# Odd tiles' x turned by VectorE and DRAM instead of TensorE, with the order around it changed, in a one-core Mamba2 layer

## What is computed

```python
xn = _layernorm(x, axis=-1)                      # x: 2 x 512 x 512
s = _L0_attn_ref(xn, in_proj_w, conv_w, conv_b, dt_bias, D, norm_w, out_proj_w)
g = _silu(_L0_ffn_ref(xn, w1, s1, w2, s2, w3, s3))
x = x + s * g
```

```python
xBC = jax.nn.silu(conv)                          # conv over the last 4 tokens
x, Bm, Cm = jnp.split(xBC, [INTER, INTER + NG * SS], axis=-1)
xdt = xc * dtc[..., None]
scores = jnp.einsum('bclhn,bcshn->bchls', Cc, Bc) * Lmat
Ydiag = jnp.einsum('bchls,bcshp->bclhp', scores, xdt)
states = jnp.einsum('bclhn,bchl,bclhp->bchpn', Bc, decay_states, xdt)
Yoff = jnp.einsum('bclhn,bchpn,bchl->bclhp', Cc, prev, jnp.exp(cs))
Y = (Ydiag + Yoff).reshape(Bsz, S, H, P) + x * D[None, None, :, None]
yg = y * jax.nn.silu(gate)
rstd = jax.lax.rsqrt(jnp.mean(jnp.square(yg_g), axis=-1, keepdims=True) + EPS)
```

## Time and profile before

| | |
|---|---|
| median of 3 runs | 1759.31 us (1758.42 to 1759.45) |
| the profiled execution | 1758.21 us, span of the core 1756.4 us |
| granted TensorE clock | 1.00 in the whole span |
| busy of the span | PE 99%, DVE 80%, ACT 70%, POOL 70% |
| DMA | 202.8 MB, mean 115 GB/s; SP's queue takes 34.8% of the 16 DMA engines |

### The profile page before, as it was taken

The page is one execution under the profiler, slowest core; times in us unless marked ns, Lnnn a source line. Parts: engine busy times, 40 slices in busy tenths (PEclk is TensorE's granted clock), DMA queues, the critical chain, the costliest instruction groups (busy, mean ns, idle before and its releaser), DMA issues.

```text
span 1756.4 us, 30305 instructions
## 1 busy us (share of the span) xinstructions
PE 1742.4 (99%) x10301; PEld 1459.3 (83%) x10301; DVE 1402.7 (80%) x2211; ACT 1221.6 (70%) x2456; POOL 1232.1 (70%) x877
## 2 busy tenths in 40 slices
PE   8999999999999999999999999999999999999999
PEld 6788888888888888888888888888888888888877
DVE  7978788878878788778788788878887887868941
ACT  6986677777776777777867778767877787643320
POOL 5677777777876787677776777677777787576630
PEclk9999999999999999999999999999999999999999
DMA  5442333333333343333333333333323343236522
GB/s 196 165 131 99 116 116 112 98 123 109 134 105 94 104 135 109 108 101 117 118 102 118 116 111 108 103 109 127 123 91 103 109 135 107 76 98 175 146 78 96
DMA packets 122595, 202.84 MB, mean 115 GB/s; under 512 B 23056, under 2 KB 60560, under 8 KB 122192
## 3 DMA queue, kind: packets, MB, share of 16 engines
q1 hardware_dynamic: 120720, 197.32, 34.8%
q10 hardware_dynamic: 1728, 3.65, 0.5%
HBM read 193.57 MB, written 7.34 MB: 114 GB/s over the span
## 4 chain that ended last, share of the span: by engine, by line
PE 94%; DVE 3%; issue 1%; POOL 1%; DMA 0%; ACT 0%; SPq 0%; DVEq 0%; ACTq 0%; POOLq 0%
PE bank L143 17%; PE bank L145 16%; PE bank L144 16%; PE bank L573 10%; PE bank L609 7%; PE bank L677 7%; PE bank L679 7%; PE bank L678 6%; PE bank L888 3%; PE bank L738 3%; DVE z L1246 1%; PE bank L700 0%; DVE lm L1267 0%; PE bank L720 0%; DVE acc L1337 0%
## 5 line engine op out<-in xcount | busy, mean ns | idle before, releaser
L964 ACT ACTIVATE lm<-lm,hp 128x128 f32<-128x128 f32 x1024 | 313.1, 389 | 0.8
L1246 DVE SCALAR_TENSOR_TENSOR z<-bank,cw_all,z 128x511 f32<-128x511 f32 (+2 forms) x384 | 286.9, 747 | 13.3 <-ACT z L1000 4.2
L1611 POOL TENSOR_TENSOR conv_lo<-raw_x,conv_hi 128x512 fp32r<-128x512 f32 x124 | 203.7, 1643 | 129.4 <-ACT conv_hi L901 129.3
L143 PE MATMUL bank<-xn_hi,conv_hi 128*128 128x512 f32 x640 | 261.4, 408 | 1.9 <-DVE z L1246 1.4
L1306 DVE TENSOR_TENSOR xdt<-bank,hp 128x512 f32<-128x512 f32 x128 | 88.2, 689 | 212.4 <-PE bank L738 212.4
L145 PE MATMUL bank<-xn_hi,conv_lo 128*128 128x512 f32 x640 | 250.6, 392 | 0.0
L144 PE MATMUL bank<-xn_lo,conv_hi 128*128 128x512 f32 x640 | 249.5, 390 | 0.0
L1594 POOL TENSOR_TENSOR yt<-yt,ec 128x384 f32<-128x384 f32 x128 | 146.8, 1147 | 139.3 <-DVE ec L1315 107.9
L1280 DVE SCALAR_TENSOR_TENSOR lm<-lm,gm 128x1024 f32<-128x1024 f32 x128 | 225.3, 1760 | 7.8 <-ACT lm L964 7.2
L1578 POOL TENSOR_TENSOR y_lo<-yt,y_hi 128x512 fp32r<-128x512 f32 x128 | 180.1, 1407 | 52.4 <-ACT y_hi L1035 52.4
L143 PE MATMUL bank<-xn_hi,gate_hi 128*128 128x512 f32 x512 | 212.9, 416 | 0.0
(11 more groups left out here) (152 smaller groups left out, 4051.5 us busy)
## 6 DMA issues: line engine op xcount, KB each, us to landing
lm<-cs_d SPq DMA_DIRECT2D x128, 512.0 KB, 4.5
raw_x<-w_conv_dram SPq DMA_DIRECT2D x128, 256.0 KB, 3.5
ec<-e_d SPq DMA_DIRECT2D x256, 96.0 KB, 2.7
raw_o<-w_out_dram SPq DMA_DIRECT2D x64, 256.0 KB, 3.0
raw_g<-w_gate_dram SPq DMA_DIRECT2D x61, 256.0 KB, 3.2
raw_g<-w_conv_dram SPq DMA_DIRECT2D x16, 256.0 KB, 3.2
raw_o<-w_conv_dram SPq DMA_DIRECT2D x14, 256.0 KB, 3.4
q_raw<-w1q_dram SPq DMA_DIRECT2D x10, 256.0 KB, 3.9
```

Source lines behind the costliest of these rows:

```text
L143: pe.matmul(dst, a_hi, b_hi, start=(i == 0), stop=False)
L964: e = act.activation(lm[m % LM_BUFS][:, u, :], lm[m % LM_BUFS][:, u, :], ACT.Exp, bias=hp[bd.seq][:, Q_CS, k1, u:u + 1])
L1246: dve.scalar_tensor_tensor(dst[:, d:SEQ], src[:, 0:SEQ - d], cw_all[:, bd.group, pos, 3 - d:4 - d], dst[:, d:SEQ], ALU.mult, ALU.add).then ...
L1611: pool.tensor_tensor(conv_lo[kx % 2][:, :, :], raw_x[:, kx % 2, :].rearrange("p (k j) -> p k j", k=KT), conv_hi[kx % 2][:, :, :].bitcast(F ...
```

## The change

Odd tiles from 7 to 123 (`by_blocks`) no longer go through `turn_x`. In step n - 2 DVE transposes the tile's `xt` in 32x32 blocks into `z[:, 1]`, SP stores that to a DRAM tensor `xb_d`, and in the step ahead of the tile's own SP loads it back in four DMAs of 32 partitions, in pieces of 32 floats, straight into `xdt[1]`, now with tokens on partitions. DVE computes `xw` from it and then scales it in place. In these odd steps t0 comes first on DVE and `scores` last, and PE's second diagonal waits for the state instead of `xw`. ACT waits for the store before it writes `z[:, 1]` anew. `sum_squares` moves from the end of step 0 to behind `y_off` of step 1, and the sums by token on DVE behind the block transpose of that step.

```diff
--- before.py
+++ after.py
@@ -47,6 +47,7 @@
 MREST = HIDDEN - MT * P
 
 LM_BUFS = 4
+BLK = P // 32
 
 SH = 4
 Q_BUFS = (2, 1, 1)
@@ -111,6 +112,16 @@
     return TILES // 2 <= n < TILES * (BODIES - 1) + TILES // 2
 
 
+def by_blocks(t):
+
+    return paired(t) and t % 2 == 1 and t >= TILES - 1
+
+
+def blocks_before(t):
+
+    return sum(1 for u in range(t) if by_blocks(u))
+
+
 def group_exists(group):
     return not isinstance(group, int) or 0 <= group < GROUPS
 
@@ -164,6 +175,7 @@
     cs_d = nc.dram_tensor("cs_d", (SEQS, HEADS, SEQ), F32).ap()
     e_d = nc.dram_tensor("e_d", (SEQS, HEADS, SEQ), F32).ap()
     hp_d = nc.dram_tensor("hp_d", (SEQS, P, NQ, GROUPS, TILES, 2 * NC), F32).ap()
+    xb_d = nc.dram_tensor("xb_d", (BLK, 32, NC, BLK, 32), F32).ap()
     mamba_d = nc.dram_tensor("mamba_d", (TT, P, DIM), F32).ap()
 
     with ExitStack() as ctx:
@@ -314,6 +326,7 @@
         ss_mm, rs_done, rv_done = sem("ss_mm"), sem("rs_done"), sem("rv_done")
         red_done = sem("red_done")
         tx_done = sem("tx_done")
+        blk_done, xb_out, xtok_in = sem("blk_done"), sem("xb_out"), sem("xtok_in")
         xdt_done, xw_done = sem("xdt_done"), sem("xw_done")
         min_done, exp_done, sc_done = sem("min_done"), sem("exp_done"), sem("sc_done")
         yd_done, yo_done = sem("yd_done"), sem("yo_done")
@@ -431,8 +444,23 @@
                                  cs_d[bd.seq, GH * bd.group + 2 * kr:GH * bd.group + 2 * kr + 2, :]
                                  .partition_broadcast(P)).then_inc(row_in[m % LM_BUFS], 16)
 
+            def blocks_out(t):
+                if by_blocks(t):
+                    sp.wait_ge(blk_done, blocks_before(t) + 1)
+                    wait(sp, xtok_in, 16 * BLK * blocks_before(t))
+                    sp.dma_start(xb_d.rearrange("g i c b j -> (g i) (c b j)"), z[:, 1, :]).then_inc(xb_out, 16)
+
+            def tokens_in(t):
+                if by_blocks(t):
+                    sp.wait_ge(xb_out, 16 * (blocks_before(t) + 1))
+                    sp.wait_ge(yd_done, t - 1)
+                    for b in range(BLK):
+                        sp.dma_start(xdt[1][32 * b:32 * b + 32, :].rearrange("i (c g j) -> i c g j", c=NC, g=BLK),
+                                     xb_d[:, :, :, b].rearrange("g i c j -> i c g j")).then_inc(xtok_in, 16)
+
             def step(body, k):
 
+                n = TILES * body.n + k
                 bx, kx = at(body, k, 5)
                 if bx.exists():
 
@@ -443,6 +471,7 @@
                 if k == 3 and nx.exists() and body.n > 0:
                     load_hp(nx)
                 load_rows(body, k)
+                blocks_out(n + 2)
                 bd, ke = at(body, k, 1)
                 if bd.exists():
 
@@ -453,6 +482,7 @@
                         sp.dma_start(ec[ke % 2][HD * j:HD * j + HD, :],
                                      e_d[bd.seq, GH * bd.group + 2 * ke + j, CHUNK:SEQ].partition_broadcast(HD)
                                      ).then_inc(ec_in[ke % 2], 16)
+                tokens_in(n + 1)
                 bd, k1 = at(body, k, 1)
                 for group, pos in out_piece(bd, k1):
                     wait(sp, wlo_o, TILES * group + pos)
@@ -615,7 +645,10 @@
                 n = TILES * body.n + k
                 pe.wait_ge(t0_done, n)
                 diag(n - 1, ps_y)
-                pe.wait_ge(xw_done, n + 1)
+                if by_blocks(n):
+                    pe.wait_ge(st_done, n)
+                else:
+                    pe.wait_ge(xw_done, n + 1)
                 diag(n, ps_x)
 
             def y_diag(body, k):
@@ -709,7 +742,7 @@
                         pe.wait_ge(t0_done, TILES * BODIES)
                         up(0, 0, P, 1, 1, 0)
                     if body.exists():
-                        wait(pe, gev_done, TILES * body.n + k + 3)
+                        wait(pe, gev_done, TILES * body.n + 3)
                     else:
                         wait(pe, st_done, TILES * BODIES)
                     if before.is_number(0):
@@ -731,7 +764,7 @@
             def turn_x(body, k):
                 n = TILES * body.n + k
                 bd, k1 = at(body, k, 1)
-                if bd.exists():
+                if bd.exists() and not by_blocks(n + 1):
                     pe.wait_ge(xs_done, TILES * bd.n + k1 + 1)
                     wait(pe, st_done, n + 1)
                     for c in range(NC):
@@ -740,6 +773,8 @@
 
             def step(body, k):
                 y_off(body, k)
+                if k == 1 and body.exists():
+                    sum_squares(body, 0)
                 conv(body, k)
                 if paired(TILES * body.n + k) and k % 2 == 0:
                     state_mm(body, k)
@@ -778,7 +813,8 @@
                     out_mm(body, k)
                 extra(body, k)
                 turn_x(body, k)
-                sum_squares(body, k)
+                if not body.exists():
+                    sum_squares(body, k)
 
             def turn(t):
                 pe.wait_ge(xn_done, t + 1)
@@ -997,6 +1033,8 @@
                     pos = X_POS[kx]
                     act.wait_ge(xp_done, m + 1)
                     wait(act, xs_done, m - 1)
+                    if by_blocks(m - 2):
+                        act.wait_ge(xb_out, 16 * (blocks_before(m - 2) + 1))
                     act.activation(z[:, kx % 2, :], ps_a[:, :], ACT.Identity, scale=cw_all[:, bd.group, pos, 3:4],
                                    bias=cw_all[:, bd.group, pos, 4:5]).then_inc(tap0_x, 1)
 
@@ -1286,8 +1324,8 @@
                 pv, kp = at(body, k, -1)
 
                 before = body.plus(-1)
-                if k == 1 and before.exists():
-
+
+                def sums_by_token():
                     dve.wait_ge(ss_mm, before.n + 1)
                     wait(dve, rv_done, before.n)
                     if body.exists():
@@ -1297,23 +1335,44 @@
                     dve.tensor_scalar(rstd_sum[:, :], tok_sum[:, :] if body.exists() else sums(before)[:, 0:NC], EPS,
                                       None, ALU.add).then_inc(rs_done, 1)
 
-                if body.exists():
-
-                    dve.wait_ge(tx_done, n + 1)
-                    if k == 0:
-                        wait_hp(dve, body)
-                    wait(dve, yd_done, n - 1)
-                    dve.tensor_tensor(by_head(xdt[n % 2][:, :]), by_head(ps_x[:, :]),
-                                      per_token(hp[body.seq], Q_DT, k, NC), ALU.mult).then_inc(xdt_done, 1)
-                    wait(dve, st_mm, n)
-                    dve.tensor_tensor(by_head(xw[:, :]), by_head(ps_x[:, 0:(NC - 1) * P]),
-                                      per_token(hp[body.seq], Q_DEC, k, NC - 1), ALU.mult).then_inc(xw_done, 1)
-                if pv.exists():
-
+                def decayed():
                     dve.wait_ge(yo_done, n)
                     dve.wait_ge(ec_in[kp % 2], 32 * (TILES // 2 * pv.n + kp // 2 + 1))
                     dve.tensor_tensor(ec[kp % 2][:, :], ps_y[:, P:NC * P], ec[kp % 2][:, :], ALU.mult
                                       ).then_inc(t0_done, 1)
+
+                if k == 1 and before.exists() and not body.exists():
+                    sums_by_token()
+                if by_blocks(n):
+                    decayed()
+
+                if body.exists():
+
+                    if by_blocks(n):
+                        dve.wait_ge(xtok_in, 16 * BLK * (blocks_before(n) + 1))
+                        dve.wait_ge(st_mm, n)
+                        dve.tensor_tensor(by_head(xw[:, :]), by_head(xdt[1][:, 0:(NC - 1) * P]),
+                                          per_token(hp[body.seq], Q_DEC, k, NC - 1), ALU.mult).then_inc(xw_done, 1)
+                        dve.wait_ge(xw_done, n + 1)
+                        dve.tensor_tensor(by_head(xdt[1][:, :]), by_head(xdt[1][:, :]),
+                                          per_token(hp[body.seq], Q_DT, k, NC), ALU.mult).then_inc(xdt_done, 1)
+                    else:
+                        dve.wait_ge(tx_done, n + 1 - blocks_before(n))
+                        if k == 0:
+                            wait_hp(dve, body)
+                        wait(dve, yd_done, n - 1)
+                        dve.tensor_tensor(by_head(xdt[n % 2][:, :]), by_head(ps_x[:, :]),
+                                          per_token(hp[body.seq], Q_DT, k, NC), ALU.mult).then_inc(xdt_done, 1)
+                        wait(dve, st_mm, n)
+                        dve.tensor_tensor(by_head(xw[:, :]), by_head(ps_x[:, 0:(NC - 1) * P]),
+                                          per_token(hp[body.seq], Q_DEC, k, NC - 1), ALU.mult).then_inc(xw_done, 1)
+                if pv.exists() and not by_blocks(n):
+                    decayed()
+                if by_blocks(n + 2):
+                    dve.wait_ge(xs_done, n + 3)
+                    dve.transpose(z[:, 1, :], xt[:, (k + 2) % 4, :]).then_inc(blk_done, 1)
+                if k == 1 and before.exists() and body.exists():
+                    sums_by_token()
 
```

(1 more changed line is left out.)

## The result

| | before | after |
|---|---|---|
| median | 1759.38 us (16 runs) | 1762.61 us (16 runs, 1761.4 to 1766.27) |
| ratio | | 1.0021, 95% interval 1.0013 to 1.0028 |
| profiled execution, span | 1758.21, 1756.4 us | 1766.27, 1764.5 us |
| TensorE clock granted | 1.00 | 0.998 |

The change makes the kernel 3.2 us slower, where 11 us less were forecast. The profiled execution of after is the longest of its 16: its preparation took 4.1 us more than in the profile of before (first `y_off` at 58.27 us instead of 54.22, with a granted clock of 0.93 in the first 16 us and 0.85 in the next 16, and 1.00 behind). From the second `y_off` to the last, that is over the main loop, it is 1510.0 us against 1506.0, near the 3.2 us of the medians.

What follows compares the result with a forecast made beforehand. PE (TensorE), busy 1742 of 1756 us, was taken to bound the kernel. 25.8 us won less 2.8, 1.6 and 10.5 lost gave 10.9 us off, a median of 1748 us, range 1734 to 1767.

Steps and rivals of the forecast that it cites:

- The gain: PE: four transposes less in each of 59 by_blocks tiles, 0.4375 us a tile, 25.8 us off the span.
- The transpose's order of size: DVE's block transpose in odd steps, in no row: taken as 0.6 to 0.65 us, bounds 0.5 and 1.4.
- The squares' move: Squares' transposes go behind y_off of step 1: the same 0.44 us, nothing gained or lost on PE.
- The path through DRAM: Store and four loads of 128 B pieces: DVE doesn't wait, cost nothing; at 60 ns a piece, 1.3 us in most odd steps.
- Step 3's arithmetic: Convolution of step 3 has 0.5 us spare, 0.44 of it goes; DVE's lateness in step 2 is lost nearly one for one.
- The full bodies' steps 1, 3 and 4: Full (even-numbered) bodies: DVE-POOL collision in step 1, its lateness returned in step 3, 1.5 us in 7 bodies, 10.5 us.
- Light bodies' step 3: Convolution of step 3 in odd-numbered bodies: scores end about 0.2 us late, 8 x 0.2 = 1.6 us lost.
- the term of step 5: Every body's gate product waits for DVE's taps of c: 1.0 us spare becomes -0.2, 14 bodies, 2.8 us lost.
- The step 1 term: Full bodies: xw and xdt collide with POOL in step 1; 1.25 to 2.25 us lost with step 3, taken as 1.5.
- The 0.25 us at the first diagonals and the 0.5 at the gate product: Full bodies' step 1: PE waits 0.25 us for xdt, then 0.5 more for the sums by token.
- DVE too full: Rival: the transpose takes a double pass, or collisions also come in even steps; 1756 to 1768 us, chance 0.20.
- Late blocks: Rival: 128 B pieces cost over about 50 ns or loads wait for one another; 1799 us at 60 ns, chance 0.10.

Runs made afterwards that it cites:

- e6: Kernel before with only the squares' transposes moved behind y_off of step 1 and the sums by token behind t0: 1758.97 us, ratio 0.9999.
- e4: Changed kernel, with POOL waiting for xdt before the low part of the convolution weights in odd steps with blocks: 1748.93 us, 0.9942.
- e1: Changed kernel, but xw and xdt read PSUM bank ps_x instead of the blocks (result not valid); store, loads and block transpose kept: 1740.55 us, 0.9891.
- e2: e1 without block transpose, store and loads; PE transposes gone and nothing in their place: 1737.97 us, 0.9881.
- e7: Changed kernel with e3 and e4 together, transpose later and POOL's wait: 1741.50 us, 0.9899.
- e12: e7 with POOL's wait for xdt in step 5 alone: 1742.41 us, 0.9904.
- e3: Changed kernel with the block transpose moved down on DVE, behind the taps of b and c and the sums by token: 1753.44 us, 0.9967.
- e8: e7 with the squares' transposes behind step 1's convolution, token sums later, and POOL's step 0 sum of squares behind the split weights: 1749.02 us, 0.9945.
- e5: Kernel before with only DVE's order of the odd steps changed, t0 first and scores last: 1757.94 us, 0.9998.

## Why the prediction was wrong

**Right.** The gain, 25.8 us: the steps 2 and 6 show it to 0.01 us a tile. The transpose's order of size: 0.70 us against 0.6 to 0.65 taken. The squares' move: nothing by itself (e6). The path through DRAM costs DVE no wait, with more margin than worked out: the four loads go out in 2.63 us and land 2.6 us after issue each (median), that is some 6.3 us behind the issue of `ec`, where 7.6 were forecast. One reason is that the 30 ns for a 256 B piece, which was worked out from a share of a window, was too high: the trace's records of single packets in the kernel before give 18 ns in the mean for 256 B and 30 for 512 B. Step 3's arithmetic (DVE's lateness in step 2 is lost on PE nearly one for one): 0.97 us in full bodies against 0.5 to 1.5. The full bodies' steps 1, 3 and 4 cost 12.4 us where 10.5 were put, with 8.75 and 15.75 as bounds. Light bodies' step 3 cost less than forecast, 0.8 us against 1.6.

**Wrong: the term of step 5.** The prediction put 14 x 0.2 = 2.8 us for the wait of the gate product on the taps of c; it measured 14 x 1.2 = 16.8. These 14 us are the miss, 10.9 + 3.2; what the other terms lack and have too much nearly cancels. The arithmetic on lateness was sound, as e4 shows: with `xdt` at 0.69 us the loss is 0.16 us a body. What failed is that the collision, priced by rule and rows for step 1 of full bodies, was put at nothing in step 5 without a look at POOL there. The earlier trace rows hold DVE and PE in step 5, but not POOL. In the kernel before `conv_lo` starts there as soon as ACT has rounded the weights, some 1.4 us behind `y_off`, where it lengthened nothing on DVE. In after it starts at 1.6 to 1.9 us, and with t0 put first `xdt` starts at 1.92. It happens in every body, full or light, since `conv_lo` waits for ACT and not for POOL's other work. The rule of the Trainium skill (SBUF — State Buffer, Who interferes with whom) that the prediction weighed was the right one, and the trace agrees: 1.78 us are the rest of POOL's instruction, 1.23, and 0.55 more. It was applied at one place instead of at each of the four odd steps. With 1.0 us more in 14 bodies the sum would have been 10.9 - 14, that is 3 us slower: the result.

**The step 1 term was near in size and partly wrong in cause.** It put 1.5 us for full bodies' steps 1 and 3, and 1.77 were lost in steps 1, 3 and 4. Of these the collision accounts for 1.01 (e1 against after: 0.21 in step 1, 0.61 in step 3 and 0.19 in step 4). The 0.25 us at the first diagonals and the 0.5 at the gate product did not occur; that 0.60 were lost in step 1 all the same, at its last transposes, is luck. The rest is, as argued above, the chain through POOL, SP and ACT; what is left in step 3 of e2 (0.33 us) has no run that explains it.

**The rivals.** "DVE too full" named 1756 to 1768 and held the time, for another reason than its own: neither did the transpose take a double pass, nor did collisions in even steps matter. That 1762.6 us lie in the stated range of 1734 to 1767 is owed to this rival and not to the sum. Its chance of 0.20 was too small, because the search for collisions had stopped at one place. "Late blocks" is refuted: DVE never waits for the loads in after, and even twice the pieces give 1.2%, not 2.3.

## What to carry to other kernels

When an operand of VectorE moves from PSUM to SBUF beside another SBUF operand, list every GpSimd instruction that can run at that moment in every step of the loop, not only where GpSimd is busiest: the one that cost most here stood in a quiet step. The cure may be one wait on the engine that has time: GpSimd waiting for `xdt` turned a change of +0.2% into one of -0.6% (e4), and with the block transpose moved down as well into one of -1.0% (e7; e12 with the wait in step 5 alone). And where the bounding engine is made earlier by 0.4 us, each of its meeting points loses that much slack, and the next one stands right behind the first (e3, e8).

## What the runs showed of the hardware

A 32x32 block transpose of 128x512 float32 on VectorE took 697 to 709 ns, about as long as the scaling of the same size from PSUM (691). With its one SBUF input it did not lengthen in any of the 59 tiles.

Pieces of 128 B were cheap to read back. After moves 133,107 packets more than before, and the queue's share rises from 34.8% of 1756.4 us to 44.0% of 1764.5 us, some 2640 us over 16 DMA engines. The records of single packets in the trace of after give 12.8 ns in the mean for the 120,832 pieces of 128 B, 18 for pieces of 256 B and 99 for pieces of 2 KB.

POOL pays for the collisions too, but less than DVE. From e1, where the scalings read PSUM, to after POOL's busy time rises by 13 us (1249.8 to 1263.0) and DVE's by 35 (1420.5 to 1455.5). The other 18 of POOL's 31 us are not the scalings' work. `rstd` takes 1868 ns instead of 1018, 16 times, and does so in e6 as well, where only the squares' place is changed. `y_lo` took 1407 ns in the mean before and 1570 after, but it still takes 1558 in e1, and 1495 in e5, where only DVE's order is changed.
